# New issue orders on five queues for the first and last graphs of a two-layer graph network

## The reference

```python
h = relu(layernorm(x))
x = x + einsum('bij,bjf->bif', L, h @ W + b)         # L: adj + I, scaled by row-sum ** -0.5 on both sides
h = relu(layernorm(x))
H = (adj != 0);  w = adj[:, 0, :]
P = B^-1-scaled H H^T;  D = 1 / (H @ w)
g = layernorm(relu(D * (P @ (h @ W1^T)) + b1)) * gamma + beta
x = x + D * (P @ (g @ W2^T)) + b2 + h
```

## Time and profile before

| what | value |
|---|---|
| median of the runs shown | 1989.09 us |
| the profiled execution's own time | 1990.53 us |
| its span in the trace | 1988.7 us |
| TensorE (PE) busy | 1956.6 us, 98% |
| VectorE (DVE), ScalarE (ACT), GpSimd (POOL) busy | 87%, 55%, 63% |
| granted TensorE clock, mean of the span | 0.998 |

### The profile page before, as it was taken

One profiled execution on the slowest core, in us unless ns is written; L12 is line 12 of the kernel. 1 busy time (PEld: TensorE's weight loads), 2 busy tenths in 40 slices (PEclk: granted clock), 3 DMA queues, 4 the chain that ended last, 5 costly groups with the idle time before them and its releaser, 6 DMA issues.

```text
span 1988.7 us, 42836 instructions
## 1 busy us (share of the span) xinstructions
PE 1956.6 (98%) x10390; PEld 949.8 (48%) x10390; DVE 1724.4 (87%) x4514; ACT 1091.4 (55%) x2099; POOL 1246.7 (63%) x1934
## 2 busy tenths in 40 slices
PE   5999999999999999999999999999999999999998
PEld 2444444444444444444444444444444444444443
DVE  7898888888888888888888888888888888888885
ACT  7555555555555555555555555555555555555553
POOL 4566666666666666666666666666666666666553
PEclk9999999999999999999999999999999999999999
DMA  5344334333433443343343334334433433433432
...
DMA packets 467951, 182.90 MB, mean 92 GB/s; under 512 B 416336, under 2 KB 432720, under 8 KB 467920
## 3 DMA queue, kind: packets, MB, share of 16 engines
q1 hardware_dynamic: 467920, 182.55, 40.1%
...
## 4 chain that ended last, share of the span: by engine, by line
PE 96%; DVE 1%; issue 1%; DMA 1%; ACT 0%; POOL 0%; SPq 0%; DVEq 0%; POOLq 0%; ACTq 0%
PE ps_c L405 33%; PE ps_u L405 33%; PE ps_e L405 16%; PE ps_e L428 1%; PE ps_c L394 1%; PE ps_c L393 1%; PE ps_c L392 1%; PE ps_e L430 1%; PE ps_e L429 1%; PE ps_y L428 1%; PE ps_y L430 1%; PE ps_y L429 1%; PE ps_a L463 1%; PE ps_p L471 0%; PE ps_p L472 0%
## 5 line engine op out<-in xcount | busy, mean ns | idle before, releaser
L579 ACT ACTIVATE h<-z 128x512 f32<-128x512 f32 x256 | 160.9, 629 | 535.0 <-DVE z L785 534.9
L1181 POOL TENSOR_TENSOR rd<-u,neg_half 128x2 f32<-128x2 f32 x128 | 178.9, 1398 | 231.7 <-DVE y L1001 224.4
L405 PE MATMUL ps_c<-w1h,t1h 128*128 128x512 f16 x1024 | 263.7, 380 | 1.5 <-DVE t1l L945 0.9
L405 PE MATMUL ps_c<-w1l,t1h 128*128 128x512 f16 x1024 | 263.1, 379 | 0.0
L405 PE MATMUL ps_c<-w1h,t1l 128*128 128x512 f16 x1024 | 262.8, 379 | 0.0
L405 PE MATMUL ps_u<-w2h,hnT_hi 128*128 128x512 f16 x1024 | 243.6, 381 | 2.2 <-DMA hnT_hi<-hn_hi 2.2
L405 PE MATMUL ps_u<-w2l,hnT_hi 128*128 128x512 f16 x1024 | 242.0, 379 | 0.0
L405 PE MATMUL ps_u<-w2h,hnT_lo 128*128 128x512 f16 x1024 | 241.9, 379 | 0.0
L1227 POOL TENSOR_TENSOR scr<-x1b,xh 128x512 f32<-128x512 f32 x128 | 231.1, 1806 | 1.0 <-ACT xh L620 0.7
L1162 POOL TENSOR_TENSOR base<-scr,vq 128x512 f32<-128x512 f32 x128 | 224.1, 1751 | 9.3 <-ACT vq L573 5.9
L1001 DVE SCALAR_TENSOR_TENSOR y<-b_sc,rd,ps_e 128x512 f32<-128x512 f32 x128 | 95.6, 747 | 142.7 <-PE ps_e L405 142.7
...
## 6 DMA issues: line engine op xcount, KB each, us to landing
x_t<-in_x_dram SPq DMA_DIRECT2D x128, 256.0 KB, 2.7
out_dram<-out_t SPq DMA_DIRECT2D x128, 256.0 KB, 2.2
adj_t<-in_adj_dram SPq DMA_DIRECT2D x128, 64.0 KB, 2.3
...
raw_w<-in_W2T_dram SPq DMA_DIRECT2D x8, 256.0 KB, 7.7
h0T_hi<-h_hi SPq DMA_TRANSPOSE x128, 2.4
h0T_lo<-h_lo SPq DMA_TRANSPOSE x128, 2.4
hnT_hi<-hn_hi SPq DMA_TRANSPOSE x128, 3.1
```

The source lines that it names most:

```text
L405: mm = pe.matmul(ps, t[:, j * 128:(j + 1) * 128], w[:, j, cols], start=(n == 0 and j == 0), stop=(n == 2 and j == blocks - 1))
L579: act.activation(h[:, cols], z[:, cols], ACT.Relu).then_inc(s_h[n], 1)
L1181: pool.tensor_tensor(rd0[:, m, :], u0[:, m, :], neg_half[:, :], ALU.pow).then_inc(s_pp0, 1)
```

## The change

The lists of all five queues ahead of the loop and behind it are replaced by other orders of the same calls. On SP the first block of W1 and the first adjacency go out first, b's row after three blocks of W, gamma and beta earlier, and W2's blocks 7, 6 and 2 stand between the two transpositions of graph 0. On TensorE `beta_row` takes four blocks before `do_Y0(0)` and two before `do_T1(0)`, and `do_Z0(1)` stands ahead of `do_Y1a(0)`. ScalarE begins with W1's block 0. In `do_cm` one more wait is written: for the reciprocal of the graph before, which is an earlier instruction of VectorE itself and is emitted only outside the loop.

```diff
+            load_weight(1, raw_w1, W1T, range(0, 1))
+            load_adj(0)
+            load_weight(0, raw_w0, W, range(2, 3))
+            load_weight(0, raw_w0, W, range(0, 2))
             load_row(b_all, b, s_b)
-            load_weight(0, raw_w0, W, range(0, 3))
-            load_adj(0)
...
+            load_weight(2, raw_w2, W2T, range(1, 2))
+            load_adj(2)
+            load_weight(2, raw_w2, W2T, range(4, 5))
+            load_x(2)
+            load_weight(2, raw_w2, W2T, range(0, 1))
             load_weight(2, raw_w2, W2T, range(3, 4))
...
+            do_tr0h(0)
+            load_weight(2, raw_w2, W2T, range(7, 8))
+            load_weight(2, raw_w2, W2T, range(6, 7))
             load_weight(2, raw_w2, W2T, range(2, 3))
+            do_tr0l(0)
             load_weight(2, raw_w2, W2T, range(5, 6))
             load_x(3)
-            load_x(2)
-            do_tr0h(0); do_tr0l(0); do_ldA(4)
...
-            do_AT(0)
+            do_AT(0); do_P(0)
             weight_sum(0, slice(0, KI + 1))
-            do_P(0); do_AT(1); do_AT(2)
+            do_AT(1)
             weight_sum(1, slice(KI + 1, 2 * KI + 1))
-            beta_row(range(0, 2))
-            do_Y0(0); do_AT(3)
-            beta_row(range(2, 4))
-            do_Z0(0); do_P(1)
+            do_AT(2)
+            beta_row(range(0, 4))
+            do_Y0(0); do_AT(3); do_P(1)
             beta_row(range(4, 6))
+            do_Z0(0)
             weight_sum(2, slice(2 * KI + 1, 2 * KI + 1 + KH))
-            do_Y0(1); do_T1(0)
+            do_Y0(1)
             beta_row(range(6, 8)).then_inc(s_vps, 1)
-            do_Y1a(0); do_Z0(1); do_Y1b(0); do_Y0(2); do_T1(1); do_P(2); do_Z0(2); do_AT(4); do_Y1b(1)
+            do_T1(0); do_Z0(1); do_Y1a(0); do_Y1b(0); do_Y0(2); do_P(2); do_AT(4); do_T1(1); do_Z0(2)
...
+            square_sum(1, raw_w1, w1h, range(0, 1))
+            do_rsum(0)
+            square_sum(0, raw_w0, w0h, range(0, 3))
+            do_P_hi(0); do_A_hi(0)
             square_sum_b()
-            square_sum(0, raw_w0, w0h, range(0, 4))
...
             def do_cm(g, i=0):
                 m = g % 2
                 dve.wait_ge(s_ht, upto(i, g))
+                wait_apart(dve, s_bi, i, g - 1)
```

More of the change, by code:

```diff
@@ L535, in _ @@
-            steady(pe, ENG.PE, step)
[L536 to L540, removed]
@@ L541, in _ @@
-            do_Y2(NG - 6); do_Z0(NG - 3); do_P(NG - 3); do_Y1b(NG - 4); do_AT(NG - 1); do_U(NG - 5)
-            do_T1(NG - 3); do_Y0(NG - 2); do_P(NG - 2); do_Y2(NG - 5); do_Y1a(NG - 3); do_Z0(NG - 2)
-            do_Y1b(NG - 3); do_U(NG - 4); do_T1(NG - 2); do_Y0(NG - 1); do_P(NG - 1); do_Y1a(NG - 2)
+            do_T1(0); do_Z0(1); do_Y1a(0); do_Y1b(0); do_Y0(2); do_P(2); do_AT(4); do_T1(1); do_Z0(2)
+            do_Y1b(1); do_Y1a(1); do_U(0); do_T1(2); do_Y0(3); do_Y1b(2); do_P(3); do_AT(5); do_Y2(0)
@@ new lines, in _ @@
+            do_Z0(3); do_Y1a(2); do_U(1); do_T1(3); do_Y0(4); do_Y1a(3); do_P(4); do_Y2(1); do_Z0(4)
+            do_Y1b(3); do_AT(6); do_Y0(5); do_U(2); do_T1(4); do_AT(7); do_P(5); do_Z0(5); do_Y2(2); do_Y1a(4)
+            do_Y1b(4); do_U(3)
+            steady(pe, ENG.PE, step)
+            do_T1(NG - 7); do_Y0(NG - 6); do_Y1b(NG - 7); do_AT(NG - 4); do_P(NG - 6); do_Y1a(NG - 7)
+            do_Z0(NG - 6); do_Y2(NG - 9); do_U(NG - 8); do_T1(NG - 6); do_Y0(NG - 5); do_P(NG - 5)
+            do_AT(NG - 3); do_Y1a(NG - 6); do_Z0(NG - 5); do_Y1b(NG - 6); do_Y0(NG - 4); do_U(NG - 7)
@@ new lines, in _ @@
+            do_T1(NG - 5); do_Y2(NG - 8); do_AT(NG - 2); do_P(NG - 4); do_Z0(NG - 4); do_Y1a(NG - 5)
+            do_Y1b(NG - 5); do_Y2(NG - 7); do_U(NG - 6); do_T1(NG - 4); do_Y0(NG - 3); do_Y1a(NG - 4)
+            do_Y2(NG - 6); do_Z0(NG - 3); do_AT(NG - 1); do_P(NG - 3); do_Y1b(NG - 4); do_U(NG - 5)
+            do_T1(NG - 3); do_Y0(NG - 2); do_Y1a(NG - 3); do_Z0(NG - 2); do_P(NG - 2); do_Y1b(NG - 3)
+            do_Y2(NG - 5); do_U(NG - 4); do_T1(NG - 2); do_Y0(NG - 1); do_P(NG - 1); do_Y1a(NG - 2)
@@ L1088, in _ @@
-            do_w_lo(3); do_ahat(3); do_cm(3); do_t1l(1); do_hn(0)
-            split_lo(2, raw_w2, w2h, w2l, range(5, 6))
-            do_hn_lo(0); do_x1(2); do_dm(2); do_ri(2); do_st1(2); do_dds(4); do_h0_lo(3); do_aggr1(2)
-            split_lo(2, raw_w2, w2h, w2l, range(6, 7))
-            do_aggr0(4); do_u0(4); do_dds(5); do_zb(1)
-            split_lo(2, raw_w2, w2h, w2l, range(7, 8))
-            do_P_lo(2); do_za(1); do_bn0(5); do_xh_lo(2); do_s2a(1); do_s2b(1); do_aggr0(5); do_aggr2(1)
@@ L1141, in _ @@
-            do_out(NG - 3); do_ul(NG - 2); do_out(NG - 2); do_ul(NG - 1); do_out(NG - 1)
+            do_zb(0); do_s2a(0); do_ahat(3); do_s2b(0); do_yv(2); do_xh_lo(1); do_aggr2(0)
+            split_lo(2, raw_w2, w2h, w2l, range(3, 5))
+            do_yl(2); do_t1l(1); do_hn(0); do_aggr0(4); do_dds(4); do_hn_lo(0); do_A_lo(3); do_h0_lo(3)
+            do_u0(4); do_dm(2); do_inv(3); do_x1(2)
+            split_lo(2, raw_w2, w2h, w2l, range(5, 6))
+            do_zb(1); do_st1(2); do_ri(2); do_aggr1(2); do_dn(2); do_za(1)
@@ new lines, in _ @@
+            split_lo(2, raw_w2, w2h, w2l, range(6, 8))
+            do_P_lo(2); do_s2b(1); do_s2a(1); do_w_hi(4); do_xh_lo(2); do_ahat(4); do_HB_hi(3); do_HT(4)
+            do_HB_lo(3); do_aggr2(1); do_bn0(5); do_t1l(2); do_ul(0); do_h0_lo(4); do_yv(3); do_hn(1)
+            do_w_lo(4); do_yl(3); do_hn_lo(1); do_zb(2); do_aggr0(5); do_bn0(6); do_x1(3); do_st1(3)
+            do_w_hi(5); do_aggr0(6); do_HT(5); do_aggr1(3); do_dm(3); do_za(2); do_A_lo(4); do_dds(5)
+            do_cm(4); do_ahat(5); do_s2b(2); do_u0(5); do_P_lo(3); do_w_lo(5); do_s2a(2); do_ri(3); do_dds(6)
```

300 lines of the change are left out of this document (141 added, 159 removed).

## The result

The changed kernel took 1994.23 us (median of 8 runs, 1992.59 to 1996.50) against 1989.24 for the kernel before beside it (8 runs, 1988.11 to 1990.66): ratio 1.0024, 95% interval 1.0015 to 1.0034. It is 5 us slower; the prediction said 1.6 faster. The profiled execution's own time is 1995.57 us, its span 1993.7.

What follows compares the result with a forecast made beforehand. TensorE, busy 98% of the span, was taken to bound the kernel, so only the two ends could move: +0.3 + 0 - 1.9 + 0 = -1.6 us, giving 1987.5 us in the runs' terms, range 1982 to 1993.

Steps and rivals of the forecast that it cites:

- The first product: `do_Y0(0)` at TensorE's start: to end at 28.4 instead of 25.4 us, 3.0 later, after waiting for W2's block 2.
- the half-way value: `beta_row`'s blocks 2 and 3 ahead of `do_Y0(0)`: taken as 2.9 us, between 1.88 (upper clock) and 3.78 (lower).
- From there to `do_Y1b(1)`: the lateness shrinks to 0.3 us.: From the end of `do_Y0(0)` to `do_Y1b(1)`: 3.0 us late becomes 0.3, starting at 52.3 instead of 51.99; bounds -2 and +3.
- The lower clock behind the gap: Matmuls at 50 to 56 us, where the lower clock cost 1.6 us: no change, bounds -1.6 and +1.6.
- The three waits ahead of the mark: TensorE's waits before `do_U(3)` starts: -2.4 us, one of 0.5 in their place, sum -1.9; bounds -2.4 and 0.
- the new wait: At `do_T1(3)`: xh's low half done some 0.5 us after `do_U(1)` ends, so 0.5 us lost.
- What that mark gains or loses, the whole kernel does.: The start of `do_U(3)`, 106.69 us before, near 105.1 predicted: its shift was to be the whole kernel's.
- the end: Behind the loop: last eight TensorE steps and VectorE's last are the same, so 0 us, bounds -1 and +1.
- The slower one: Block 2 lands at 26.2 us, product 4.8 behind forecast, second lower-clock stretch costs 1.6: 1993.9 us; chance 0.13.
- The start did not run through: Rival: block 2 lands at 22.4 us, upper clock from there, product ends at 26.9: 1983.9 us; chance 0.28.
- Nothing arrives: Rival: early loss and late gain cancel, closed gaps reappear in front of other steps: 1989.1 us; chance 0.17.
- X-bar: DMA transpositions at the start: the skill's rule would make block 2 and the time 0.8 us earlier; rows speak against it.

Runs made afterwards that it cites:

- the kernel with `scr` moved: Changed kernel with GpSimd's scr2 of graph 5 put back ahead of three one-column instructions: 1994.42 us, ratio 1.0023 to the kernel before.
- block 2 early: Changed kernel with SP's load of W2's block 2 issued ahead of the first transposition: 1992.22 us, ratio 1.0012 to the kernel before.
- The block-2 kernels: Changed kernel with W2's block 2 loaded ahead of the first transposition, 1992.22 us; or with `beta_row`'s blocks 2 and 3 behind `do_Y0(0)`, 4 and 5 behind `do_Z0(0)`, 1991.81.
- SP's swap alone: Kernel before with SP's transposition of graph 2's high half ahead of its low half and the load of x(8): 1987.65 us, ratio 0.9990.
- the kernel with all repairs of the start: Changed kernel with W2's block 2 loaded before the first transposition, GpSimd's scr2(5) moved back, W2's block 7 rounded before `do_hb(1)`, old end: 1989.01 us, ratio 0.9997.

## Why the prediction was wrong, point by point

- **The first product.** `do_h0_hi(0)` came at 16.62 (16.7 predicted), the transposition's issue at 17.50 (17.6). TensorE resumed on block 2 at 23.76 (22.8): 3.9 us from its issue, between the two rows taken as ends. The blocks behind the pause took 3.78 us, the length of the lower level of the clock throughout, where I had taken 2.9; the first four matmuls of the product 1.44 instead of 1.03. The product ended at 30.3: the term is 5.1 instead of 3.0. By the rule of the Trainium skill ("TensorE: Matmul & The Clock Gate", Part 1: the engine is throttled unless it is kept active) I had worked out 30.4, and this trace agrees with it; the kernel with `scr` moved, the same up to there, has the pause too and ended the product at 28.28, near my 28.4. So the half-way value was a mean of two outcomes: in the three profiled executions with this start and this pause the blocks took 3.78, 3.78 and 1.98 us, nothing between.
- **"From there to `do_Y1b(1)`: the lateness shrinks to 0.3 us."** This step failed whatever the clock did. I had the lateness shrink by 2.7 us; it shrank by 0.9, from 5.1 to 4.2, and in the kernel with `scr` moved, where the product was only 3.1 late, to 2.5. From the product's end to `do_T1(0)` it was 10.3 us instead of my 9.3 (10.5 before), with block 2 early too. I had counted on two VectorE splits of W1 leaving that chain. One left, and y's low half began 1.54 us behind y instead of 1.86. The other is still there, beside GpSimd's `sc` and `nm`, which the chain waits for. VectorE and GpSimd, before and then now:

```profile
31.92 1.25 DVE L773 SCALAR_TENSOR_TENSOR w1l<-raw_w,wsc,w1h 128x1024 f16<-128x1024 f32 x1
32.00 1.30 POOL L1213 TENSOR_SCALAR nm<-st,sc 128x1 f32<-128x1 f32 x1 [0.17 <-POOL sc L1207]
```

```profile
35.92 1.25 DVE L775 SCALAR_TENSOR_TENSOR w1l<-raw_w,wsc,w1h 128x1024 f16<-128x1024 f32 x1
35.97 1.61 POOL L1210 TENSOR_TENSOR sc<-u,neg_half 128x1 f32<-128x1 f32 x1
```

  The two GpSimd operations took 0.55 and 1.30 us before and 1.61 and 0.27 now, the same in sum. From `do_T1(0)` to `do_Y1b(1)` it was 15.6 us (16.3 before, 14.6 predicted): `do_T1(1)` came 2.2 us behind the end of `do_Y0(2)` where I had 1.3, waiting for `xh_lo`. The block-2 kernels begin `do_Y1b(1)` at 52.22 and 52.38, so nearly all of the 4.2 is the product's delay handed on.
- **The lower clock behind the gap: 0.** Right: 1.91 and 1.50 us against 1.91 and 1.39. It is no fixed price: with block 2 early the same eight took 1.03 and 1.03.
- **The three waits ahead of the mark: -2.4, +0.5.** Right in sum: `do_U(0)` to `do_U(3)` 2.15 us shorter (-1.9 predicted), though the new wait stood at `do_T1(2)`, for 0.29 us, and not at `do_T1(3)`. In the kernel before, SP's swap alone gave 1.4 in the profile and 2.0 in the timed runs, and with graph 8's statistics later 2.2 and 3.0.
- **"What that mark gains or loses, the whole kernel does."** Wrong twice, and the largest miss of all, 2.9 us in the profile. The same set of steps was issued on TensorE, but VectorE came to the loop with more left (15.48 us of work between `do_U(3)` and `do_U(4)` instead of 12.44), which cost 1.2 us behind the mark. And the end, taken as 0 because TensorE's last steps are the same, lost 1.7 in the profile and 2.8 in the timed runs: I compared TensorE's last steps and only the last rows of VectorE's, and passed over VectorE's middle of that list, where it stands idle for 2 us already in the kernel before and where the new order puts `hn` and other work ahead of `xh_lo`.
- **The rivals.** The slower one named 1993.9, near the measured 1994.2, but not by its own way: its condition, a landing at 25.5 or later, was not met, and no second lower-clock stretch was added. The start did not run through, and with block 2 early, where it did up to 27 us, the gain ended at the next wait. "Nothing arrives" named what the kernel with all repairs of the start did, 1989.01 us, where closed gaps came back ahead of other steps; the change itself did worse than that.
- **X-bar.** The Trainium skill ("Advanced Engine Details and Errata", X-Bar Transpose: as fast as regular transfers) would have put block 2 earlier still; it came 1 us later than my value. The issue of the transposition took 1.29 us again, and that of the three copies behind it 1.51 together.

In sum: +5.1 (product), -0.9 (to `do_Y1b(1)`), +0.1 (clock), -2.15 (waits), +1.2 (first iteration), +1.7 (end) = 5.0 us, the spans' difference, where I had +3.0, -2.7, 0, -1.9, 0, 0. It closes for these two executions; 2 us of the first term are the clock of one of them, and the timed runs put the start at 2.0 us and the end at 2.8, each known to some 1.8.
